# Dequantisation spread on through layer 2's experts, with their inner activations kept by halves of the tokens in a ring of three

## The chip, the core and the metric

The kernel runs on one core of a Trainium2 chip. The metric is the time of one execution on the device, in microseconds (us); lower is better. The engines of a core run each their own instruction stream and wait for each other through semaphores: TensorE (PE, matmuls), VectorE (DVE), ScalarE (ACT), GpSimd (POOL) and SyncE (SP, which here only issues DMA transfers).

## What is computed

A stack of four layers on x of 4 x 256 tokens x 512. Each layer adds a cross-attention to a context of 4 x 64 tokens and then a feed-forward part. The two parts that matter here are layer 2's mixture of three experts and layer 3's feed-forward, whose weights are first quantised to NF4 and dequantised:

```python
# layer 2, feed-forward: all three experts, for all tokens
pre = einsum('bsd,edf->ebsf', h, w1) + b1
act = stack([tanh(pre[0]), gelu(pre[1]), silu(pre[2])])
expert_out = einsum('ebsf,efd->ebsd', act, w2) + b2
# two of them are chosen for each batch and weighed for each token

# layer 3, feed-forward: for each of w1, w2 (1376 x 512), w3 (512 x 1376)
flat = w.reshape(-1, 64)
absmax = max(abs(flat), axis=1)
idx = searchsorted(bounds, flat / absmax)
dq = NF4_CODE[idx] * absmax
h = silu(x @ dq1.T) * (x @ dq2.T)
out = h @ dq3.T
```

The other parts are attention of 16 heads in layer 0, a ternary FFN in layer 0, attention straight to the context in layers 1 and 2, a routed low-rank FFN in layer 1, and attention of 32 heads in layer 3.

## The kernel before

All tokens stay in SBUF as eight tiles of 128 (x), and as a transposed copy in two parts, high and low (xT), in two halves of 512 tokens. A product of full precision is three passes over the high and low parts. So a product of a 512-deep contraction with 128 x 512 outputs is 12 matmuls (L1636). PE writes to a round of seven PSUM banks; an eighth, NF_BANK, belongs to the dequantisation.

`schedule()` writes out one list of steps. Every engine walks this list and does its own part of each step, in order, so an engine that waits holds back all that stands behind it in its stream. Steps named here: `scores0`, `turn0`, `pv0` and `q0` are layer 0's attention; `up0` and `down0` its FFN; `stats` normalises half of x on DVE (L1141 to L1163) and `turn` transposes it on PE (L1661), with a copy of the high part on ACT and the low part on DVE. `gate2` and `moe` make the experts' gates. `hid2(e, c, hf)` is one product of expert e: chunk c of 128 inner features, half hf of the tokens. ACT applies the function into `hf2` (L1048), DVE casts it into `h2` (L1464) and POOL subtracts for the low part (L820). `out2(e, t)` is the second product for token tile t, which DVE adds to x with the gate's factor (L1472, L1473). `k3`, `v3` and `q3` begin layer 3; ACT copies k3 and v3 out of PSUM (L893). `turn(6, hf)` needs the small weight lnw, which POOL loads in `stats(6, 1)`.

The dequantisation of layer 3's weights is independent of x and runs as background. 33 jobs `nf_max` find the block maxima of row tiles (L1550). Then 33 items (three matrices, eleven tiles each) are done. For each, SP loads the weights and the broadcast maxima and reciprocals (`nf_load`, L765 and L767), DVE scales (L1575) and does 15 steps `nf` (L1581, one comparison times a constant each, into a ring of six buffers `nf_y`), PE sums them by 15 matmuls `nf_sum` (L1977) into NF_BANK, four steps behind, DVE closes the item (`nf_end`, L1591) and SP stores it to DRAM (`nf_store`, L773).

`with_background()` inserts these jobs between the first step `v0` and the first step whose name is BACKGROUND_END, in proportion to `room()` of the steps passed: each `nf` costs 1 and each `nf_max` 1.2, and room() is the time that a product leaves, as a table says (2.6 for a product of 12 full matmuls). Weights come through `staging` to a ring of five `slots`: SP loads a chunk two ahead of its split, ACT makes the high part (L903) and POOL the low part (L813). SP issues these loads, the item loads and the stores in one queue.

The tensors of the later stages share memory: h2 and the small tensors of the gate lie where the dequantisation's buffers were. So gate2 and the small loads before it wait until the last item is stored.

## Time and profile before

| | us |
|---|---|
| median of the runs (3, 1707.07 to 1708.24) | 1707.35 |
| the profiled execution | 1711.2 |
| its span, first to last instruction | 1709.4 |
| PE busy | 1443.9 |
| DVE busy | 1083.9 |
| ACT busy | 458.6 |
| POOL busy | 296.5 |

The mean granted clock of TensorE is 0.893 of full speed. Ends of matmuls are modelled in the records, so a busy PE isn't always a PE at its peak. The chain that ended last is followed back from the last instruction, at each step to what released it; its shares say on which engine and line the time of a stretch stands. A line of the form `start us, us, engine line op out<-in xcount [idle before <-releaser]` is a piece of the timeline.

### The profile page before, as it was taken

What the parts mean: (1) busy time and instruction counts of PE and PEld (TensorE: products, weight loads), DVE (VectorE), ACT (ScalarE), POOL (GpSimd) and SP (SyncE); (2) the same over time, 40 slices, a digit from 0 to 9 for tenths busy, and PEclk for the clock granted to TensorE, in tenths of its full rate; (3) what the DMA queues carried; (4) which work ended last, traced back from release to release, by engine and by line L of the source; (5) the groups of instructions that cost most, each with busy time, mean ns of one, the idle gap of its engine ahead of it and who ended that gap; (6) DMA issues with size and microseconds to landing.
All of it is one profiled execution on the core that took longest, in us unless ns stands there. A gap on an engine that the chain in (4) does not pass through costs nothing.

```text
span 1709.4 us, 18898 instructions
## 1 busy us (share of the span) xinstructions
PE 1443.9 (84%) x6489; PEld 1131.2 (66%) x6489; DVE 1083.9 (63%) x2489; ACT 458.6 (27%) x994; POOL 296.5 (17%) x170
## 2 busy tenths in 40 slices
PE   6569999998999898899646878858999778789998
PEld 5347776776677667688545767747887546567786
DVE  4556876767777666948886756554446399944142
ACT  3223423332343333313131202101221333322010
POOL 4101111111111111202021002111543121012120
PEclk9779999999999999999855699557999889899999
DMA  5521232322232212222001112200112000001011
GB/s 184 159 77 46 80 82 68 82 74 58 64 89 71 75 50 69 72 66 67 25 26 46 42 40 60 63 18 1 50 49 62 26 25 1 1 27 60 16 36 49
DMA packets 99407, 96.40 MB, mean 56 GB/s; under 512 B 13138, under 2 KB 72418, under 8 KB 99314
## 3 DMA queue, kind: packets, MB, share of 16 engines
q1 hardware_dynamic: 98802, 94.35, 19.0%
q8 instruction: 54, 0.88, 0.2%
q0 software_dynamic: 512, 0.85, 0.2%
q14 instruction: 39, 0.32, 0.1%
HBM read 84.34 MB, written 10.82 MB: 56 GB/s over the span
## 4 chain that ended last, share of the span: by engine, by line
PE 62%; DVE 25%; issue 4%; ACT 4%; DMA 2%; SPq 1%; POOL 1%; DVEq 0%; ACTq 0%; POOLq 0%
PE bank L1636 48%; PE bank L1977 5%; PE bank L1728 4%; DVE nf_y L1581 3%; DVE st L1141 2%; DVE xn L1159 1%; PE bank L1661 1%; DVE xT L1118 1%; PE bank L1718 1%; DVE mx L1192 1%; DVE mx L1498 1%; ACT e L936 1%; DMA nf_w<-in_L_w 1%; DVE sm L1510 1%; SPq L767 1%
## 5 line engine op out<-in xcount | busy, mean ns | idle before, releaser
L1636 PE MATMUL bank<-xT,slots 128*128 128x512 f32 (+1 forms) x1920 | 467.6, 402 | 9.6 <-DVE xT L1118 7.8
L1636 PEld LDWEIGHTS bank<-xT,slots 128*128 128x128 f32 (+1 forms) x1920 | 354.8, 186 | 109.0 <-issue 8.9
L813 POOL TENSOR_TENSOR slots<-staging,slots 128x1024 fp32r<-128x1024 f32 (+4 forms) x97 | 230.5, 2379 | 1103.0 <-ACT slots L903 1103.0
L1581 DVE TENSOR_SCALAR nf_y<-nf_w 128x512 fp32r<-128x512 f32 (+2 forms) x495 | 232.2, 496 | 29.0 <-PE bank L1977 28.0
L1636 PE MATMUL bank<-slots,h 128*128 128x512 f32 (+1 forms) x728 | 178.8, 405 | 20.1 <-DVE h L1248 13.9
L1977 PE MATMUL bank<-nf_y,nf_d 128*128 128x512 f32 (+2 forms) x495 | 170.6, 429 | 10.3 <-DVE nf_y L1581 8.0
L1636 PEld LDWEIGHTS bank<-slots,h 128*128 128x128 f32 (+1 forms) x728 | 140.8, 194 | 56.1 <-DVE h L1248 14.8
L903 ACT ACTIVATE slots<-staging 128x1024 fp32r<-128x1024 f32 (+4 forms) x97 | 98.1, 1018 | 189.9 <-PE bank L1636 174.2
L936 ACT ACTIVATE e<-bank,mx 128x320 f32<-128x320 f32 x128 | 66.4, 523 | 271.1 <-DVE mx L1195 254.0
L1977 PEld LDWEIGHTS bank<-nf_y,nf_d 128*128 128x128 f32 (+1 forms) x495 | 95.3, 197 | 47.0 <-issue 15.5
L1214 DVE TENSOR_TENSOR x<-bank,x 128x512 f32<-128x512 f32 x72 | 49.7, 690 | 110.9 <-PE bank L1636 110.6
L1728 PE MATMUL bank<-eT,v 128*96 128x256 f32 (+1 forms) x384 | 112.0, 414 | 1.5 <-ACT eT L946 1.5
L1118 DVE TENSOR_TENSOR q<-bank,q 96x256 fp32r<-96x256 f32 (+1 forms) x96 | 48.8, 508 | 77.3 <-ACT q L888 76.8
L1636 PE MATMUL bank<-slots,q 96*128 96x512 f32 x384 | 95.3, 397 | 0.7 <-DVE q L1118 0.7
L1718 PE MATMUL bank<-ident,e 128*128 128x128 f32 x256 | 50.6, 294 | 44.5 <-ACT e L936 22.4
L1636 PEld LDWEIGHTS bank<-slots,q 96*128 96x128 f32 x384 | 71.6, 188 | 18.6 <-issue 2.1
L1728 PEld LDWEIGHTS bank<-eT,v 128*96 128x96 f32 (+1 forms) x384 | 58.2, 172 | 37.6 <-issue 25.3
L1661 PE MATMUL bank<-ident,xn 128*128 128x128 f32 x256 | 49.6, 360 | 31.9 <-DVE xn L1159 31.6
L1636 PE MATMUL bank<-k,q 96*128 96x320 f32 x384 | 69.6, 317 | 5.7 <-ACT e L936 4.4
L1718 PEld LDWEIGHTS bank<-ident,e 128*128 128x128 f32 x256 | 35.0, 151 | 53.7 <-ACT e L936 30.6
L1636 PEld LDWEIGHTS bank<-k,q 96*128 96x128 f32 x384 | 61.9, 192 | 13.0 <-ACT e L936 4.7
L1661 PEld LDWEIGHTS bank<-ident,xn 128*128 128x128 f32 x256 | 42.8, 189 | 39.2 <-issue 34.7
(246 smaller groups left out, 1897.8 us busy)
## 6 DMA issues: line engine op xcount, KB each, us to landing
staging<-in_L_wqkT SPq DMA_DIRECT2D x16, 480.0 KB, 3.8
nf_out<-nf_w SPq DMA_DIRECT2D x30, 256.0 KB, 2.1
staging<-nf_out SPq DMA_DIRECT2D x30, 256.0 KB, 2.8
staging<-in_L_woT SPq DMA_DIRECT2D x16, 384.0 KB, 3.5
staging<-in_L_w SPq DMA_DIRECT2D x12, 512.0 KB, 4.0
nf_a<-nf_max SPq DMA_DIRECT2D x40, 128.0 KB, 3.6
nf_r<-nf_rcp SPq DMA_DIRECT2D x40, 128.0 KB, 3.4
nf_w<-in_L_w SPq DMA_DIRECT2D x15, 256.0 KB, 4.4
```

What stands on the lines that cost most here:

```text
L813: g.tensor_tensor(lo, split_source(i), hi.bitcast(FP32), ALU.subtract).then_inc(*sig.mark("weight_low", i))
L903: sc.activation(weight(name, 0), split_source(i), ACT.Copy).then_inc(*sig.mark("weight_high", i))
L936: sc.activation(e0[:, (2 * n + i) % E0_RING], psum(("scores0", n, i))[:, 0:KEYS0], ACT.Exp, scale=HD0 ** -0.5, bias=mx[:, n % 4, 2 + i:3 + ...
L1118: v.tensor_tensor(dst, src, hi.bitcast(FP32), ALU.subtract).then_inc(*sig.mark(f"{stage}_low", key))
L1141: ins = v.bn_stats(st[:, t], x[:, t])
L1214: v.tensor_tensor(x[:, t], src, x[:, t], ALU.add).then_inc(*sig.mark(*mark))
L1581: v.tensor_scalar(nf_y[0:rows, i % STAIR_RING, 0:size], w_, bound, first, compare, ALU.mult)\
L1636: ins = mm(dst, l_, r_, start=i == 0, stop=i == len(passes) - 1)
L1661: ins = nc.tensor.transpose(bank[:, i * P:(i + 1) * P], xn[:, i, c * P:(c + 1) * P], ident[:])
L1718: nc.tensor.transpose(b0[:, (2 * k + i) * P:(2 * k + i + 1) * P], e0[:, (2 * n + i) % E0_RING, k * P:(k + 1) * P], ident[:])
L1728: ins = mm(bank[0:HD0, 0:S], v0[0:p, t, g * HD0:(g + 1) * HD0], eT0[0:p, n % 2, k], start=k == 0, stop=k == 2)
L1977: mm(banks[NF_BANK][0:rows, 0:size], nf_d[0:rows, j - 1, 0:rows], nf_y[0:rows, i % STAIR_RING, 0:size], start=j == 1, stop=j == NPART).the ...
```

## The change

BACKGROUND_END becomes "k3": the jobs are spread from v0 to the end of the experts, over more steps and so more thinly. The dequantisation's buffers live until then; the tensors of layer 3's attention take their place. Hence the waits for the last nf4 store move from gate2 (ACT, DVE) and from the small loads (POOL) to `k3(0)` on ACT and to the load of lnw on POOL. h2 no longer fits with both parts of two experts for all tokens. It holds three halves: slot (2e + hf) mod 3. The experts' steps are grouped by half: first the hid2 of (0, 0), (0, 1) and (1, 0), then an out2 group of four tiles, then the next hid2 group, and so on. DVE's cast of group r waits for the out2 group r - 3.

```diff
-BACKGROUND_END = "gate2"
+H2_RING = 3
+BACKGROUND_END = "k3"
...
-    steps += [("hid2", 0, 0, 0), ("turn", 5, 1), ("hid2", 0, 0, 1)]
+    steps += [("hid2", 0, 0, 0), ("turn", 5, 1), ("hid2", 0, 1, 0)]
     steps += [("gate2", t) for t in range(TPH, TILES)]
-    for i in range(2 * (KT - 1)):
-        steps += [("moe", i)] * (i < 4) + [("hid2", 0, 1 + i // 2, i % 2)]
-    steps += [("hid2", 1, c, hf) for c in range(KT) for hf in range(2)]
-    for e in range(MOE):
-        steps += [("out2", e, t) for t in range(TPH)]
-        if e == MOE - 1:
+    hidden = [[("hid2", e, c, hf) for c in range(KT)] for e in range(MOE) for hf in range(2)]
+    outer = [[("out2", e, t) for t in range(hf * TPH, (hf + 1) * TPH)] for e in range(MOE) for hf in range(2)]
+    for i, s in enumerate(hidden[0][2:] + hidden[1]):
+        steps += [("moe", i)] * (i < 4) + [s]
+    steps += hidden[2]
+    for i, s in enumerate(outer):
+        steps += s + (hidden[i + H2_RING] if i + H2_RING < len(hidden) else [])
+        if i == len(outer) - 2:
             steps.append(("stats", 6, 0))
-        steps += [("out2", e, t) for t in range(TPH, TILES)]
-        if e + 2 < MOE:
-            steps += [("hid2", e + 2, c, hf) for c in range(KT) for hf in range(2)]
...
-        nfs.close()
...
-        h2 = sb("h2", [P, 2, 2, KT, TOK], F32R, l)
+        h2 = sb("h2", [P, H2_RING, 2, KT, HALF], F32R, l)
...
+        nfs.close()
...
                 elif kind == "stats" and args == (5, 1):
...
-                    for q in range(2):
-                        pool.wait_ge(*sig.when(f"nf4_stored{q}", 3 * FT - 2 + (3 * FT - q) % 2))
...
                 elif kind == "stats" and args == (6, 1):
...
+                    for q in range(2):
+                        pool.wait_ge(*sig.when(f"nf4_stored{q}", 3 * FT - 2 + (3 * FT - q) % 2))
                     small_loads([], [("lnw", lnw[:], a["L3_lnw"])])
...
             def k3_(c):
+                if c == 0:
+                    for q in range(2):
+                        act.wait_ge(*sig.when(f"nf4_stored{q}", 3 * FT - 2 + (3 * FT - q) % 2))
                 keep("k3", c, kr3[:, c], psum(("k3", c))[:, 0:B * CTX])
...
             def hid2(e, c, hf):
-                i = (e * KT + c) * 2 + hf
+                i, r = hid2_no(e, c, hf), 2 * e + hf
                 dve.wait_ge(*sig.when("hid2_value", (e, c, hf)))
-                if e >= 2:
-                    dve.wait_ge(*sig.when("out2_product", (e - 2, TILES - 1)))
-                v.tensor_copy(h2[:, e % 2, 0, c, hf * HALF:(hf + 1) * HALF], hf2[:, i % 2])\
+                if r >= H2_RING:
+                    e_, h_ = divmod(r - H2_RING, 2)
+                    dve.wait_ge(*sig.when("out2_product", (e_, (h_ + 1) * TPH - 1)))
+                v.tensor_copy(h2[:, r % H2_RING, 0, c], hf2[:, i % 2])\
                     .then_inc(*sig.mark("h2_high", (e, c, hf)))
```

The lines of the changed kernel stand two to four further down: L1977 is L1980 there, L1581 is L1583, L1636 is L1638.

PE around the gate (`gw,xT` is gate2, `nf_y,nf_d` a background sum, `ctxN,eT` the end of layer 2's attention), before:

```order
L1790 MATMUL bank<-ident,e 64x128 x2
L1636 MATMUL bank<-ctxN,eT 128x512 x6
L1977 MATMUL bank<-nf_y,nf_d 96x512 x6
L1636 MATMUL bank<-gw,xT 128x4 x48
L1636 MATMUL bank<-xT,slots 128x512 x12
L1661 MATMUL bank<-ident,xn 128x128 x16
```

and with the change:

```order
L1638 MATMUL bank<-ctxN,eT 128x512 x6
L1980 MATMUL bank<-nf_y,nf_d 128x512
L1638 MATMUL bank<-gw,xT 128x4 x12
L1980 MATMUL bank<-nf_y,nf_d 128x512
L1638 MATMUL bank<-gw,xT 128x4 x12
L1980 MATMUL bank<-nf_y,nf_d 128x512
L1638 MATMUL bank<-gw,xT 128x4 x12
L1980 MATMUL bank<-nf_y,nf_d 128x512
L1638 MATMUL bank<-gw,xT 128x4 x12
L1980 MATMUL bank<-nf_y,nf_d 128x512
L1638 MATMUL bank<-xT,slots 128x512 x12
L1980 MATMUL bank<-nf_y,nf_d 128x512 x2
```

The six sums that stood before the gate are one, and sums stand between the gate's products from there on.

PE at the end of the experts (`slots,h` is out2, `ctxT,slots` k3, `slots,ctxT` v3, `ident,xn` turn(6, 0)), before:

```order
L1636 MATMUL bank<-xT,slots 128x512 x96
L1636 MATMUL bank<-slots,h 128x512 x192
L1636 MATMUL bank<-ctxT,slots 128x256 x48
L1636 MATMUL bank<-slots,ctxT 64x128 x48
L1661 MATMUL bank<-ident,xn 128x128 x16
```

and with the change, from the sums ahead of out2(2, 6) on:

```order
L1980 MATMUL bank<-nf_y,nf_d 96x512 x2
L1638 MATMUL bank<-slots,h 128x512 x12
L1980 MATMUL bank<-nf_y,nf_d 96x512 x2
L1638 MATMUL bank<-slots,h 128x512 x12
L1980 MATMUL bank<-nf_y,nf_d 96x512 x6
L1638 MATMUL bank<-ctxT,slots 128x256 x48
L1638 MATMUL bank<-slots,ctxT 64x128 x48
L1663 MATMUL bank<-ident,xn 128x128 x16
```

Six sums stand between the last product of out2 and k3.

DVE at the same place (`y<-bank,b2b` and `x<-y,cf,x` add one out2 tile, `rt<-x` reports that half of x is done), before, from out2(2, 6) on:

```order
L1472 TENSOR_TENSOR y<-bank,b2b 128x512
L1473 SCALAR_TENSOR_TENSOR x<-y,cf,x 128x512
L1472 TENSOR_TENSOR y<-bank,b2b 128x512
L1473 SCALAR_TENSOR_TENSOR x<-y,cf,x 128x512
L1229 COPY rt<-x 1x1
L1172 SCALAR_TENSOR_TENSOR xT<-bank,lnw,xT 128x512 x4
```

and with the change:

```order
L1583 TENSOR_SCALAR nf_y<-nf_w 96x512 x2
L1474 TENSOR_TENSOR y<-bank,b2b 128x512
L1475 SCALAR_TENSOR_TENSOR x<-y,cf,x 128x512
L1583 TENSOR_SCALAR nf_y<-nf_w 96x512 x2
L1474 TENSOR_TENSOR y<-bank,b2b 128x512
L1475 SCALAR_TENSOR_TENSOR x<-y,cf,x 128x512
L1232 COPY rt<-x 1x1
L1583 TENSOR_SCALAR nf_y<-nf_w 96x512
L1593 SCALAR_TENSOR_TENSOR nf_w<-bank,nf_a 96x4x128
L1175 SCALAR_TENSOR_TENSOR xT<-bank,lnw,xT 128x512 x4
```

Two background steps stand before each add, one step and the item's last operation behind the report and before the turn.

## Rows read from the trace of the kernel before

**Rows 1.** The page's first line: the span.

```profile
span 1709.4 us, 18898 instructions
```

**Rows 2.** Busy time of each engine by stretch: attention, then experts.

```profile
core 0: us, PE busy (x) PEld busy (x) DVE busy (x) ACT busy (x) POOL busy (x), PEclk, DMA share, GB/s
135.00:640.00 505.00, 476.73 (x2304) 357.03 (x2303) 364.05 (x877) 179.40 (x483) 73.93 (x31) 0.98 0.26 71
1200.00:1300.00 100.00, 100.00 (x436) 81.42 (x435) 44.85 (x56) 23.41 (x29) 46.16 (x28) 1.00 0.17 53
```

**Rows 3.** The same view for L1581, the background step, alone (x count).

```profile
135.00:640.00 505.00, 161.60 (x326) 0.98 0.26 71
640.00:800.00 160.00, 24.32 (x65) 0.95 0.25 70
800.00:1134.00 334.00, 42.04 (x93) 0.72 0.14 40
```

**Rows 4.** The chain that ended last, shares by line, in the same four stretches.

```profile
by line: PE bank L1636 12.0%; DMA nf_w<-in_L_w 10.5%; POOL slots L813 6.8%; DVE nf_m L1550 5.7%; PE bank L1728 5.2%; DMA nf_a<-in_L_w 4.6%; issue 3.9%; DMA x<-in_x 3.3%; PE bank L1661 3.2%; DVE mx L1192 2.9%; ACT slots L903 2.9%; DVE st L11
...
by line: PE bank L1636 40.2%; PE bank L1728 11.7%; PE bank L1977 11.4%; DVE nf_y L1581 6.9%; PE bank L1718 3.3%; DVE mx L1192 2.9%; issue 2.9%; ACT e L936 2.7%; SPq L767 2.0%; DVE mx L1195 2.0%; DVE q L1118 1.9%; ACT q L888 1.8%; PE bank L1
...
by line: PE bank L1636 78.2%; PE bank L1977 9.1%; issue 3.0%; DVE xT L1118 1.6%; DVE xn L1159 1.0%; DVE f L1237 0.9%; DVE f L1236 0.9%; DVE f L1238 0.9%; DVE st L1141 0.7%; ACT slots L903 0.6%; DVE f L1235 0.5%; DVE f L1260 0.4%; ACT f L967
...
by line: PE bank L1636 36.0%; issue 5.6%; DVE nf_y L1581 5.2%; PE bank L1977 4.5%; DVE st L1141 4.3%; DVE xT L1118 3.6%; DVE xn L1159 3.1%; PE bank L1661 2.6%; DVE f L1236 2.1%; DVE f L1238 2.1%; DVE f L1237 2.1%; PE bank L1829 1.8%; DVE f 
```

**Rows 5.** SP's queue in time; DVE's waits, 135 to 640 us.

```profile
569.97 5.87 SPq L767 DMA_DIRECT2D nf_a<-nf_max  x10
...
DVE nf_w L1575 <- DMA nf_r<-nf_rcp: 14.2, 6, 4.7
```

**Rows 6.** Instructions in time (start, us), 1130 to 1165 us, before the experts.

```profile
1130.78 2.87 PE L1977 MATMUL bank<-nf_y,nf_d 96*96 96x512 f32 x6
...
1131.62 0.14 DVE L1229 COPY rt<-x 1x1 f32<-1x1 f32 x1
...
1134.60 2.44 DVE L1141 BATCH_NORM_STATS2 st<-x 128x6 f32<-128x512 f32 x4
...
1164.23 0.94 PE L1636 MATMUL bank<-xT,slots 128*128 128x512 f32 x3 [2.24 <-DVE xT L1118]
```

**Rows 7.** PE in time; groups (busy, mean ns); durations (ns, minimum/median/maximum).

```profile
1221.43 22.56 PE L1636 MATMUL bank<-slots,h 128*128 128x512 f32 x96
...
L820 POOL TENSOR_TENSOR h<-hf,h 128x512 fp32r<-128x512 f32 x24 | 30.8, 1285 | 64.2 <-DVE h L1464 64.2
...
L1473 DVE SCALAR_TENSOR_TENSOR x<-y,cf,x 128x512 f32<-128x512 f32 x24 | 27.1, 1128 | 0.8
...
L1464 DVE CAST h<-hf 128x512 fp32r<-128x512 f32 x24 | 15.1, 627 | 50.7 <-ACT hf L1048 50.7
...
L1473 DVE SCALAR_TENSOR_TENSOR x<-y,cf,x x24: 752/752/2427, 1225.2 to 1320.1; 128x512 f32<-128x512 f32 x24
...
L1581 DVE TENSOR_SCALAR nf_y<-nf_w 128x512 fp32r<-128x512 f32 x326 | 161.7, 519 | 10.7 <-PE bank L1977 9.9
...
L1581 DVE TENSOR_SCALAR nf_y<-nf_w x495: 337/417/2581, 120.5 to 1131.7; 128x512 fp32r<-128x512 f32 x150, 128x384 fp32r<-128x384 f32 x10, 96x512 fp32r<-96x512 f32 x5
```

**Rows 8.** Instructions in time, end of the experts, 1300 to 1326 us.

```profile
1300.94 0.14 DVE L1229 COPY rt<-x 1x1 f32<-1x1 f32 x1
...
1310.43 6.16 PE L1636 MATMUL bank<-ctxT,slots 128*128 128x256 f32 x48
...
1314.92 0.69 DVE L1472 TENSOR_TENSOR y<-bank,b2b 128x512 f32<-128x512 f32 x1
...
1319.34 0.91 PE L1636 MATMUL bank<-slots,ctxT 128*64 128x128 f32 x12 [0.71 <-DVE x L1473]
...
1322.21 0.14 DVE L1229 COPY rt<-x 1x1 f32<-1x1 f32 x1
...
1325.42 2.72 ACT L888 ACTIVATE xT<-bank,lnw 128x512 fp32r<-128x512 f32 x4 [1.11 <-DMA lnw<-in_L_lnw]
```

More of the change, by code:

```diff
@@ L683, in stair, with hid2_no @@
             return n * NPART + j - 1
+        def hid2_no(e, c, hf):
+            return (2 * e + hf) * KT + c
         def nf_size(m, f):
@@ L817, in hid2 @@
                 pool.wait_ge(*sig.when("h2_high", (e, c, hf)))
-                i = (e * KT + c) * 2 + hf
-                cs = slice(hf * HALF, (hf + 1) * HALF)
-                g.tensor_tensor(h2[:, e % 2, 1, c, cs], hf2[:, i % 2], h2[:, e % 2, 0, c, cs].bitcast(FP32),
-                                ALU.subtract).then_inc(*sig.mark("h2_low", (e, c, hf)))
+                i, h = hid2_no(e, c, hf), h2[:, (2 * e + hf) % H2_RING]
+                g.tensor_tensor(h[:, 1, c], hf2[:, i % 2], h[:, 0, c].bitcast(FP32), ALU.subtract).then_inc(*sig.mark("h2_low", (e, c, hf)))
             def keys3(n, b, c):
@@ L1027, in gate2 @@
                 if t == 0:
-                    for q in range(2):
-                        act.wait_ge(*sig.when(f"nf4_stored{q}", 3 * FT - 2 + (3 * FT - q) % 2))
                     act.wait_ge(*sig.when("pool_gate", "pad"))
@@ L1040, in hid2 @@
             def hid2(e, c, hf):
-                i = (e * KT + c) * 2 + hf
+                i = hid2_no(e, c, hf)
                 act.wait_ge(*sig.when("hid2_product", (e, c, hf)))
@@ L1044, in hid2 @@
                 if i >= 2:
-                    e_, r_ = divmod(i - 2, 2 * KT)
-                    act.wait_ge(*sig.when("h2_low", (e_, r_ // 2, r_ % 2)))
+                    r_, c_ = divmod(i - 2, KT)
+                    act.wait_ge(*sig.when("h2_low", (r_ // 2, c_, r_ % 2)))
                 func = (ACT.Tanh, ACT.Gelu, ACT.Silu)[e]
@@ L1379, in gate2 @@
                 if t == 0:
-                    for q in range(2):
-                        dve.wait_ge(*sig.when(f"nf4_stored{q}", 3 * FT - 2 + (3 * FT - q) % 2))
                     dve.wait_ge(*sig.when("gw_high", 0))
@@ L1893, in out2 @@
                 bank = claim(("out2", e, t), ("out2_added", (e, t)))
-                pairs = [([h2[:, e % 2, q, k, t * P:(t + 1) * P] for q in range(2)], [w[k // 2][q][:, k % 2] for q in range(2)])
+                h, i = h2[:, (2 * e + t // TPH) % H2_RING], t % TPH
+                pairs = [([h[:, q, k, i * P:(i + 1) * P] for q in range(2)], [w[k // 2][q][:, k % 2] for q in range(2)])
                          for k in range(KT)]
```

1 line of the change is left out of this document (removed).

## The prediction

> **What bounds the kernel now.** The profiled execution took 1711.2 us, its span is 1709.4 us [rows 1], and the median of the runs is 1707.35 us; I work out a difference against the profiled execution and subtract it from the median. I read the busy times by stretch first: layer 0's attention (135 to 640 us) has PE busy 476.73 of 505 us, DVE 364.05; the experts (1200 to 1300) have PE busy 100 of 100 us, DVE only 44.85 [rows 2]. So the idle DVE is in the experts, and so is the fullest PE. The background is a DVE step (L1581) and a PE matmul (L1977), 495 of each. It stands in the first 1134 us and nowhere later [rows 3]. Last I read its share of the chain that ended last, by stretch [rows 4].
>
> **What the change moves.** The jobs are spread in proportion to room(). The eligible steps hold 612.6 units of room before; 8 gate2 of 1.2 and 48 products of 2.6 add 134.4. The bill is 33 x 1.2 + 495 = 534.6, so density falls from 0.87 to 0.72 jobs per unit. Counted in the two programs' orders, layer 0's attention has 337 steps before and 269 after (68 fewer), the first FFN up to its second down pass 71 and 58 (13 fewer), from there to gate2 87 and 72 (15 fewer), gate2 and experts 0 and 96.
>
> **What the thinned stretches give.** The price of one step is the chain's share by the steps there. Attention: L1977 11.4%, L1581 6.9%, L767 2.0% of 505 us, together 102.5 us for 326 steps, 0.314 us each [rows 3, 4]; 68 fewer give 21.4 us. FFN: 9.1% of 160 us for 65 steps, 0.224 us; 13 give 2.9. After it: 5.2% and 4.5% of 334 us, 32.4 us for 93 steps, 0.35 us; 15 give 5.2. Sum **29.5 us**. The lower end is that a dropped step frees only its matmul: 96 in 22.56 us, 0.235 us each [rows 7], so 96 x 0.235 = 22.6 us. I take the chain's price, because DVE steps and DMA issue do stand in the chain beside the matmul.
>
> Start, 0 to 135 us: the 33 block maxima (L1550) and the row loads they wait for are 5.7 + 10.5 + 4.6% of 135 us, 28 us of chain [rows 4]. Their number stays, but 18% more real steps lie between them. 18% of 28 is **5 us**; ends 0 (the same loads are merely waited for elsewhere) and 10.
>
> Loads: an item of the third matrix is loaded by one DMA and 20 broadcasts, and ten of these take 5.87 us of issue on SP's queue, so the item takes 12 [rows 5]. The load stands 7 steps ahead of its use. A step takes 505/326 = 1.55 us now, so 10.9 us against 12 and the landing; DVE waited 14.2 us in 6 cases [rows 5]. At 269 steps it takes about 1.9 us, 13.3 us ahead. I take **4 us** beyond what the shares hold already; ends 0 and 12.
>
> Gate: x was done for its second half at 1131.62, but DVE first ended the background's last item, which waited for six sums on PE, and began stats(5,1) at 1134.60; stats starts up to **2.9 us** sooner [rows 6]. The small loads on POOL start 5 us sooner and stay hidden, since the gate's weights wait for DVE, behind stats. What follows there is the same chain. hid2 now takes the first half of the tokens again after turn(5,1), so PE's wait of 2.24 us for xT [rows 6] is covered: **2.2 us**. Together the gains are 29.5 + 5 + 4 + 2.9 + 2.2 = 43.6 us.
>
> **What the experts pay.** By the order 89 sums stand before out2(2,4), 30 of them 384 wide: 59 x 0.235 + 30 x 0.176 = **19 us** of a PE that has no gap [rows 2, 7]. Ends: 15 if some fall into waits of the gate, and 21 if the narrow ones cost as much as the wide. The first ones fall where the granted clock is low: 6 sums took 2.87 us, 0.48 each [rows 6], so some 8 of them add **2 us**. Two background steps before stats(6,0): **0.8 us**. Loads of items 29 and 32 stand three to four products ahead, about 9.5 to 13 us, against 12 to 14 us needed, and SP first waits for weight splits; PE runs on until it meets a sum of the late item: **4 us**, ends 0 and 8. The ring of three costs nothing: each h2 slot is rewritten only after a group of out2 that PE has ended already, and out2 of a half has four products between itself and the last hid2 that feeds it, some 11 us against ACT's activation, DVE's cast of 0.6 and POOL's 1.3 us [rows 7]. That cover would cost 2.5 us a group, six groups, if it were gone.
>
> End of the experts, the largest single loss. Count from 1300.94, the end of DVE's out2(2,3). Before, k3 starts on PE at 1310.43 under DVE's stats and adds, done(6,1) is at 1322.21, lnw lands, and ACT turns at 1325.42, 24.5 us after the start [rows 8]. Now six background steps (0.42 each) stand among DVE's last four adds. DVE also meets two POOL splits, which already stretched L1473 there, from its median of 0.75 us to 2.43 at most [rows 7]. So done(6,1) comes at about +24.3 instead of +21.3. Behind it stands step 15, and PE's sixth sum waits for that before k3: k3 starts at +25.2 instead of +9.5. k3 takes 6.2 us, v3 3.6, the first transposes 0.8: ACT turns at +35.7. That is **11 us** later. Queued behind the sum on PE are k3, v3 and the turn of layer 6; ACT's k3 copies and POOL's lnw load wait for the last nf4 store, at about +32, and so are not last. Ends: 6 (POOL's splits fall elsewhere) and 20 (the clock falls while PE waits).
>
> Costs: 19 + 2 + 0.8 + 4 + 11 = 36.8 us. Against 43.6 that is **7 us faster**: 1704 for the profiled execution, 1700.5 for the median.
>
> **A rule weighed.** L1581 has a median of 417 ns and a maximum of 2581 ns; its mean in the attention is 519 ns, with POOL busy 73.93 of 505 us [rows 2, 7]. In the experts POOL is busy 46.16 of 100 us.
> The Trainium skill (SBUF — State Buffer, "SBUF: two separate sides") says that VectorE and GpSimd share a port pair that one instruction holds to its end while the other is blocked. That speaks against putting background DVE steps where POOL splits h2; the stretched L1473 agrees, 2.427 us beside a median of 0.752 [rows 7]. What it would give is the second rival.
>
> **Rivals.** (1) *The waits for loads go almost wholly.* The attention and the start keep no wait for rows or broadcasts: 12 us instead of 4, 10 instead of 5: 13 us more, **1687.5**. For it: DVE waits 14.2 us for broadcasts, and 28 us of the start are chain [rows 4, 5]. Against: PE was not idle through all of it.
> (2) *DVE becomes the bound of the experts.* There it does 24 adds of 0.69 + 1.13 and 24 casts of 0.63 us [rows 7, 8], and for 6 items the scaling and the closing operation, 1.4 us by my estimate: 67 us. PE needs 48 x 2.82 + 19 = 154 us. So DVE decides once a step costs (154 - 67)/89 = 0.98 us. Scaling its excess over the median with POOL's share, 0.10 x 46/15, gives 0.73 us: below, but not by much, and casts wait in order for ACT. At 1.15 us the stage is 15 us longer: **1716**.
> (3) *The saved waits were covered.* Start and loads give nothing: 9 us lost, **1709**, no difference. For it: PE is busy 94% of the attention [rows 2].
> That the change does not do what it says is excluded by the order: 96 steps stand in the experts.
>
> **How the numbers follow.** Forecast 1700.5 with 0.40, its own range 1693 to 1706; rival 1 0.19; rival 3 0.19; rival 2 0.22. The range 1687 to 1714 cuts off half of rival 1 and the top of rival 2, 0.2 in all. About 0.2% (3.4 us) can be told from no change. Faster by more: 0.37 of the forecast's 0.40 and rival 1's 0.19, 0.56; within: 0.03 + 0.19 = 0.22; slower: 0.22.
>
> **What would show it.** The attention ends some 25 to 30 us sooner (start and loads within it). Gate to the first expert product keeps its length but for 2 us. The experts are 25 us longer, PE still full; if PE has gaps there that end at L1583 or at h2, rival 2 holds. Between the last out2 and the first q3, PE waits for DVE's last step, and k3 stands behind it. I am wrong if the thinned attention gives under 15 us, or if L1583 has a mean over 0.9 us after gate2.

## The result and the profile after

| | kernel before | changed kernel |
|---|---|---|
| median of 4 runs, us | 1707.8 (1707.07 to 1708.97) | 1735.1 (1733.94 to 1736.69) |
| profiled execution, us | 1711.2 | 1734.67 |
| its span, us | 1709.4 | 1732.9 |

The ratio is 1.016, with a 95% interval of 1.0142 to 1.0177: 27 us slower, where 7 us faster was forecast, and outside the range of 1687 to 1714. Beside three experiments in a later session the same kernel gave 1730.3 us (1724.9 to 1737.0), a ratio of 1.0125 (1.0081 to 1.0169). The sign is safe, the size uncertain by some 5 us. All medians and ratios are of executions in the faster of two states; of all runs only two of the kernel before with 2 broadcasts (1782.75 and 2367.23 us) fell in the slower one and are left out.

The page's first line, the busy time of each engine in the attention and in the experts, and then the same view for L1583 alone, the background step (L1581 before):

```profile
span 1732.9 us, 18901 instructions
...
core 0: us, PE busy (x) PEld busy (x) DVE busy (x) ACT busy (x) POOL busy (x), PEclk, DMA share, GB/s
132.00:623.00 491.00, 463.58 (x2224) 346.53 (x2223) 334.63 (x804) 178.76 (x481) 73.70 (x31) 0.96 0.24 66
1190.00:1300.00 110.00, 109.81 (x482) 89.77 (x481) 84.69 (x123) 23.74 (x29) 49.50 (x29) 1.00 0.26 69
...
132.00:623.00 491.00, 131.09 (x265) 0.96 0.24 66
623.00:790.00 167.00, 21.70 (x54) 0.94 0.20 56
790.00:1126.00 336.00, 35.68 (x76) 0.71 0.15 43
1126.00:1305.00 179.00, 60.85 (x83) 0.89 0.21 56
```

Against [rows 2, 3]: the attention has 61 steps fewer in its stretch (265 for 326), but is only 14 us shorter, and its granted clock is 0.96 instead of 0.98. In the experts TensorE is still full at the upper level of its clock, so the background costs there what its sums take.

To see where the time goes, all traces are laid on each other by TensorE's own products: every matmul that is not of the background has the same number in every kernel. The table gives when some of them start, as a difference to the kernel before, with the first one of each trace set equal. The forecast's column is its terms added up to that place; the last three columns belong to experiments below.

```
                            before,  fore-  changed  scales  tail steps  ring only,
product no., place          us       cast   kernel   first   out         scales first
 500  attention, early      171.1    -5      -6.9    -10.7   -10.0       -5.0
2250  end of attention      620.0   -30     -16.8    -26.6   -23.0       -8.5
3000  end of feed-forward   839.7   -33     -10.6    -30.6   -26.3       -8.6
3250  routers               957.6           -15.3    -34.1   -30.0       -8.2
3750  last before the gate 1096.5   -38.5    -5.9    -24.0   -19.5       -9.7
4000  experts, early       1184.8   -43.6    -6.3    -23.5   -20.2      -12.2
4500  third expert's last  1304.8   -18     +11.2     -4.7   -16.4      -12.0
4750  next layer's scores  1369.4    -7     +20.9     +6.6    -6.0      -11.9
5750  last feed-forward    1646.3    -7     +22.0     +7.8    -4.7      -10.7
```

From the experts on, the costs came out near the forecast (27 us instead of 37 from product 4000 to 4750; but 15 sums already stand between the gate and product 4000, and the gain of 5 us forecast for that stretch doesn't show there, so from product 3750 on it is 27 us instead of 32). It is the gain in front of them that is missing: 6 us instead of 38.5 at product 3750. Two places stand out, the feed-forward layer, which gives 6 us back, and the stretch from the routers to the gate, which gives back 9.

The feed-forward layer, instructions in time (start, us; in brackets the idle time before, and what ended it):

```profile
716.82 0.69 DVE L1593 SCALAR_TENSOR_TENSOR nf_w<-bank,nf_a 128x512 f32<-128x512 f32 x1 [2.36 <-PE bank L1980]
...
717.43 1.42 DVE L1583 TENSOR_SCALAR nf_y<-nf_w 128x512 fp32r<-128x512 f32 x4
717.54 0.34 SPq L777 DMA_DIRECT2D nf_out<-nf_w  x1
...
719.86 1.77 DVE L1583 TENSOR_SCALAR nf_y<-nf_w 128x512 fp32r<-128x512 f32 x5 [1.01 <-PE bank L1980]
...
721.48 0.34 SPq L769 DMA_DIRECT2D nf_w<-in_L_w3T  x1
721.87 5.84 SPq L771 DMA_DIRECT2D nf_a<-nf_max  x10
...
735.02 0.69 DVE L1577 TENSOR_TENSOR nf_w<-nf_w,nf_r 128x512 f32<-128x512 f32 x1 [9.77 <-DMA nf_r<-nf_rcp]
...
737.26 1.62 PE L1980 MATMUL bank<-nf_y,nf_d 128*128 128x512 f32 x3 [5.78 <-DVE nf_w L1593]
```

SP's queue stores an item at 717.54 and issues the load of the next third-matrix item only at 721.48, once the store has landed. Ten broadcasts of maxima take 5.84 us of issue, ten more of scales follow, and VectorE stands still for 9.77 us until the scales are there. TensorE runs dry for 5.78 us behind it. A like wait of 6.75 us is at 265 us, in the attention. The sum of VectorE's waits for scales is 28.1 us in 6 here and was 29.9 in 9 before; the kernel before has one of 8.4 us too, at 765 us. So the waits themselves don't tell what they cost, and two experiments below take them away on either schedule.

### The profile page after: what moved, and what is told of

Read it like the earlier page. It is cut to its first block, busy times and chain, and to the rows that moved or that the text cites. A ratio compares the mean times of both kernels' runs of the same rounds, so it can differ in the third digit from the quotient of the medians.

```text
span 1732.9 us, 18901 instructions
## 1 busy us (share of the span) xinstructions
PE 1459.6 (84%) x6489; PEld 1143.8 (66%) x6489; DVE 1103.8 (64%) x2489; ACT 458.7 (26%) x994; POOL 298.7 (17%) x170
## 4 chain that ended last, share of the span: by engine, by line
PE 62%; DVE 24%; issue 5%; ACT 3%; DMA 2%; SPq 2%; POOL 1%; ACTq 0%; DVEq 0%; POOLq 0%
PE bank L1638 48%; PE bank L1980 5%; PE bank L1730 4%; DVE nf_y L1583 3%; DVE st L1144 2%; SPq L771 2%; DVE xn L1162 1%; PE bank L1720 1%; PE bank L1663 1%; DVE xT L1121 1%; DVE mx L1500 1%; DVE mx L1195 1%; ACT e L938 1%; POOL slots L817 1%; DVE sm L1512 1%
## 5 line engine op out<-in xcount | busy, mean ns | idle before, releaser
L1638 PE MATMUL bank<-xT,slots 128*128 128x512 f32 (+1 forms) x1920 | 467.1, 400 | 11.0 <-DVE xT L1175 5.9
L1638 PEld LDWEIGHTS bank<-xT,slots 128*128 128x128 f32 (+1 forms) x1920 | 353.6, 185 | 110.4 <-issue 10.6
L1583 DVE TENSOR_SCALAR nf_y<-nf_w 128x512 fp32r<-128x512 f32 (+2 forms) x495 | 258.1, 545 | 29.8 <-PE bank L1980 28.7
L1638 PE MATMUL bank<-slots,h 128*128 128x512 f32 (+1 forms) x728 | 188.7, 416 | 21.3 <-DVE h L1251 15.1
L1980 PE MATMUL bank<-nf_y,nf_d 128*128 128x512 f32 (+2 forms) x495 | 174.7, 430 | 16.1 <-DVE nf_y L1583 10.3
L1638 PEld LDWEIGHTS bank<-slots,h 128*128 128x128 f32 (+1 forms) x728 | 145.5, 201 | 58.1 <-DVE h L1251 16.0
L1980 PEld LDWEIGHTS bank<-nf_y,nf_d 128*128 128x128 f32 (+1 forms) x495 | 96.4, 199 | 56.1 <-DVE nf_y L1583 22.5
L1730 PE MATMUL bank<-eT,v 128*96 128x256 f32 (+1 forms) x384 | 117.2, 430 | 1.7 <-ACT eT L948 1.7
L1638 PE MATMUL bank<-slots,q 96*128 96x512 f32 x384 | 95.1, 396 | 1.2 <-DVE q L1121 1.2
L1638 PEld LDWEIGHTS bank<-slots,q 96*128 96x128 f32 x384 | 71.8, 188 | 19.1 <-issue 2.3
L1638 PE MATMUL bank<-k,q 96*128 96x320 f32 x384 | 73.2, 328 | 10.8 <-ACT e L938 6.9
L1638 PEld LDWEIGHTS bank<-k,q 96*128 96x128 f32 x384 | 65.2, 201 | 17.7 <-ACT e L938 7.4
L1720 PEld LDWEIGHTS bank<-ident,e 128*128 128x128 f32 x256 | 36.3, 155 | 45.0 <-ACT e L938 23.6
```

The source lines that it names most:

```text
L1583: v.tensor_scalar(nf_y[0:rows, i % STAIR_RING, 0:size], w_, bound, first, compare, ALU.mult)\
L1638: ins = mm(dst, l_, r_, start=i == 0, stop=i == len(passes) - 1)
L1720: nc.tensor.transpose(b0[:, (2 * k + i) * P:(2 * k + i + 1) * P], e0[:, (2 * n + i) % E0_RING, k * P:(k + 1) * P], ident[:])
L1730: ins = mm(bank[0:HD0, 0:S], v0[0:p, t, g * HD0:(g + 1) * HD0], eT0[0:p, n % 2, k], start=k == 0, stop=k == 2)
L1980: mm(banks[NF_BANK][0:rows, 0:size], nf_d[0:rows, j - 1, 0:rows], nf_y[0:rows, i % STAIR_RING, 0:size], start=j == 1, stop=j == NPART).the ...
```

## The experiments

The experiments ran in four sessions; each gives a ratio to the kernel before on the same chip. Its medians there were 1710.6, 1708.35, 1707.7 and 1709.2 us.

### The ring alone, and the background's end alone

Both start from the changed kernel.

```
 # ring alone
-BACKGROUND_END = "k3"
+BACKGROUND_END = "gate2"
 # end at the third expert's product
-BACKGROUND_END = "k3"
+BACKGROUND_END = ("out2", 2, 0)
```

> The changed kernel with the background ending at gate2 again: the jobs stand as densely as before, the experts' steps are grouped by halves and h2 is the ring of three, the waits for the last store stand at k3. If the ring costs nothing and only the spread does, this is 1703 to 1706 us (2.2 us for the covered turn, up to 2.9 at the gate). If the grouping by halves costs PE waits on h2 or on weights, it is 1712 us or more.

Measured: 1708.4 us (1699.3 to 1711.6), ratio 0.9987 (0.9967 to 1.0008). The trace has nothing up to the gate and 5.8 us of gain behind it, where the forecast had 5.1 for the earlier stats and the covered turn. The ring costs nothing. By the medians of all its runs the gain is 2.2 us.

> The changed kernel with the background ending before out2(2, 0) instead of before k3. The end of the experts then has no background step among DVE's last adds and no sum ahead of k3. If that place costs the 12 us that the two traces show, this is 1722 to 1725 us against 1735. If the loss there comes from the grouping or from elsewhere, it stays within 3 us of 1735.

Measured: 1708.25 us (1705.5 to 1710.9), ratio 0.9982 (0.9966 to 0.9998), 27 us less than the changed kernel. By the trace none of it is gained behind the gate: from product 3750 to 4750 this version loses 28 us against the kernel before and the changed kernel 27, since six sums in one piece now cost 4.5 us ahead of the third expert's product, and the gate's stretch (product 3750 to 4000) is 5 us dearer. The whole advantage lies in front of the gate (-33.0 us at product 3750, against -6.0), where the steps stand only a little denser: 9 us of it where the wait of the feed-forward layer is missing, 7 between the routers and the gate, and 15 in the start and the attention, less 4 in between. What makes the 15 is not shown. It has three waits for scales, 15.2 us in all, and none in the feed-forward layer.

### What a background step is worth

From the kernel before, three of the fifteen steps of items 1 to 21 go, with their sums (the second expectation below says sixteen, counting the scaling):

```
+        def left_out(n, j):
+            return 1 <= n <= 21 and j in (3, 8, 13)
...
             def nf(n, m, f, j):
...
+                if left_out(n, j):
...
+                    return
...
             def nf_sum(n, m, f, j):
...
+                if left_out(n, j):
...
+                    return
```

> The kernel before with 63 background steps and their sums left out, 3 of 15 in items 1 to 21, so all in layer 0's attention; nothing is added elsewhere. The dequantised values are not the reference's. This is the thinning alone. By the chain's price of the prediction (0.31 us a step) it is 20 us faster, 1688. By the matmul's price (0.235) 15 us, 1693. If the changed kernel's small gain there is the true price (10 us for 68 steps, 0.15 each, since the clock falls when PE has fewer matmuls) it is 1698 us or more, with a mean granted clock in the attention under 0.98.

Measured: 1697.8 us (1696.9 to 1699.1), ratio 0.9928 (0.99 to 0.9955). 63 steps with their sums are worth 12.8 us, **0.20 us** each; the traces say 12.4 at the end of the attention, where the granted clock is 0.97.

The same with the second part of the edit taken back, so that TensorE makes the 63 sums of stale steps and VectorE doesn't make the steps:

> The kernel before, with the same 63 background steps of VectorE left out as in the run with fewer steps (three of the sixteen of items 1 to 21), but their 63 sums on TensorE kept. This leaves those steps out of the computation. The run with fewer steps was 1697.8 us beside 1710, so a step with its sum was worth some 0.19 us there. Theory A: TensorE sets the pace of the attention, so nearly all of that price is the sum's time on TensorE: this run comes back to 1708 to 1710. Theory B: the price is VectorE's (a step of 0.5 us delays the real VectorE work on which TensorE waits): this run stays at 1697 to 1700. In between, the price is shared in proportion.

Measured: 1709.3 us (1704.2 to 1716.2), ratio 1.0006 (0.9987 to 1.0024). The price is TensorE's, within the interval: 63 steps of VectorE less, of 0.5 us each, are worth nothing there, give or take 4 us.

### What the experts pay

From the version with scales first (below), 13 of 15 steps of items 27 to 32 and their sums are left out, so 78 in all; loads, scaling, closing operation and stores stay.

```
+        def left_out(n, j):
+            return n >= 27 and 1 < j < NPART
```

> The changed kernel with the scales loaded first, and of the last six background items (27 to 32, nearly all behind the gate) 13 of 15 steps and their sums left out, so that part of the dequantisation is not computed; loads, scalings, closing operations and stores of these items stay. It prices what the experts pay. The forecast's terms for these 78 steps: 17 us of sums, 2 for the low clock, nearly all of the 11 us at the end: 28 to 32 us below the 1719 us of the version with scales first, so 1687 to 1691. If a step among the experts costs no more than one in the attention (0.18 us) and the end goes with it, 14 + 11: 1694. If the end stays, because the store and the closing operation make it and not the steps, 1700 to 1704.

Measured: 1705.7 us (1702.1 to 1708.2), 13.1 us below the 1718.75 of that version; ratio to before 0.9977 (0.9964 to 0.999). By the table it is 15.0 us shorter from product 4000 to 4500, where 10 sums stand instead of 78 (41 of them 128x512, 30 128x384 and 7 96x512). That is **0.22 us** for each of the 68, and close to the forecast's own price: 42 wide ones at 0.235 and 26 narrow ones at 0.176 us are 14.4 us. And the end stays: from 4500 to 4750 this version loses 10.4 us, with only two steps of the last item left. The end of the experts in it, in time:

```profile
1304.61 0.40 DVE L1592 TENSOR_SCALAR nf_y<-nf_w 96x512 fp32r<-96x512 f32 x1
1305.07 0.74 PE L1993 MATMUL bank<-nf_y,nf_d 96*96 96x512 f32 x1 [10.66 <-DVE nf_y L1592]
1305.61 8.08 PE L1648 MATMUL bank<-ctxT,slots 128*128 128x256 f32 x48
...
1320.34 1.84 ACT L896 ACTIVATE xT<-bank,lnw 128x512 fp32r<-128x512 f32 x3 [3.47 <-DMA lnw<-in_L_lnw]
```

TensorE waits 10.66 us for one step that stands behind VectorE's stats and last adds, and the next layer's keys are queued behind its sum. In the changed kernel the same place reads:

```profile
1323.81 0.74 PE L1980 MATMUL bank<-nf_y,nf_d 96*96 96x512 f32 x1 [4.72 <-DVE nf_y L1583]
...
1329.65 5.02 POOL L817 TENSOR_TENSOR slots<-staging,slots 128x1024 fp32r<-128x1024 f32 x2 [25.21 <-ACT slots L905]
...
1329.97 0.14 DVE L1232 COPY rt<-x 1x1 f32<-1x1 f32 x1
1330.04 2.38 DVE L1583 TENSOR_SCALAR nf_y<-nf_w 96x512 fp32r<-96x512 f32 x1
...
1332.47 0.47 PE L1980 MATMUL bank<-nf_y,nf_d 96*96 96x512 f32 x1 [2.89 <-DVE nf_y L1583]
1332.78 7.39 PE L1638 MATMUL bank<-ctxT,slots 128*128 128x256 f32 x48
...
1339.33 1.27 ACT L895 ACTIVATE kr<-bank 128x256 f32<-128x256 f32 x4 [8.81 <-DMA nf_out<-nf_w]
...
1340.49 1.05 ACT L905 ACTIVATE slots<-staging 128x1024 fp32r<-128x1024 f32 x1
...
1341.62 2.38 POOL L817 TENSOR_TENSOR slots<-staging,slots 128x1024 fp32r<-128x1024 f32 x1 [6.96 <-ACT slots L905]
...
1342.89 1.93 PE L1663 MATMUL bank<-ident,xn 128*128 128x128 f32 x16
...
1343.94 0.56 POOL L811 DMA_DIRECT2D lnw<-in_L_lnw  x1
...
1346.96 2.42 ACT L890 ACTIVATE xT<-bank,lnw 128x512 fp32r<-128x512 f32 x4 [3.60 <-DMA lnw<-in_L_lnw]
```

The wait is spread over two sums, and the last step took 2.38 us where the median of L1583 is 0.42, beside GpSimd's splits. ACT turns 16.99 us after the mark at 1329.97, where it was 3.21 us before [rows 8]. Keys and values now stand in between, but they are not what ends last: the transposes start at 1342.89, and ACT then still waits 3.60 us for lnw. GpSimd issues that load only at 1343.94, behind a split whose high part ACT makes after its copies of k3; the copies begin when the last store has landed. The version without the steps has the same wait, 3.47 us. No run moves the load of lnw alone, so what it costs is not shown.

### The end, packed

The changed kernel's schedule; the 14 steps that stood behind the start of the third expert's product are placed directly ahead of it.

```
             base = with_background(base, "v0", BACKGROUND_END, jobs)
+            at = base.index(("out2", 2, 0))
+            late = [s for s in base[at:] if s[0].startswith("nf")]
+            base = base[:at] + late + [s for s in base[at:] if not s[0].startswith("nf")]
```

> The changed kernel, its own spacing kept up to the third expert's product; only the background work that stood from there on (14 steps, the last item's sums, its closing operation and its store) is moved directly ahead of that product. Theory of the forecast: the end of the experts is delayed by 10 to 12 us because the last step and its sums stand in front of the next layer's key product, so this run is at 1735 - 12 = 1723 us, and the first product of the next layer stands 10 us sooner against the gate than in the changed kernel. Rival: the run with the background ended there gained 27 us because of the end itself; then this one is at 1710 as well. If 1723, the other 15 us of that gain come from where the loads and steps fall in the first layer.

Measured: 1728.15 us (1726.1 to 1734.7), ratio 1.0131 (1.01 to 1.0163). It looks like 7 us, but the trace says otherwise. Up to that product it has the instructions of the changed kernel, one for one, and is already 8.6 us ahead at product 4000; then it loses 10.6 us at the packed place and gains 10.3 behind the experts. Both theories missed: a burst of the last item costs as much in front of the product as behind it. Here 21 sums stand in one piece for 13.4 us; with the end at the third expert's product and even spacing, it is six for 4.5 us, as ahead of k3 in the changed kernel. The 8.6 us are how far two executions of the same instructions can lie apart.

### Late scales

First an earlier issue of the whole load:

```
-                    if j == NPART // 2 + 1 and n + 1 < len(items):
+                    if j == 5 and n + 1 < len(items):
```

> The changed kernel with each item's load issued after step 5 of the item ahead of it instead of after step 8. If the late loads on SP's queue cost what the chain shows for L771 (some 25 to 30 us in all, in pieces of 10), this is 1715 to 1725 us. If PE would wait for other things there anyway, it is 1732 us or more.

Measured: 1731.0 us (1729.4 to 1732.3), ratio 1.0121 (1.0093 to 1.0149). Three steps more of lead gave almost nothing. VectorE's waits for scales from 132 to 1305 us (us in total, times, longest), first the changed kernel's:

```profile
DVE nf_w L1577 <- DMA nf_r<-nf_rcp: 20.0, 5, 9.8
```

and with the earlier load:

```profile
DVE nf_w L1577 <- DMA nf_r<-nf_rcp: 16.7, 3, 8.6
```

The load can't be issued earlier, since it waits on SP's queue for the landing of the store before it.

Then 2 broadcasts instead of 20 for a third-matrix item, on both kernels:

```
-                    for dr in range(4):
-                        p = 0
-                        while p < w:
...
+                    pairs.append((dst_tile[0:w, 0:D], src[0:4].partition_broadcast(w)))
```

> The changed kernel, with the scales of a third-matrix item brought by 2 broadcasts where there were 20, and so left out in part (the dequantised values are not the right ones); every other instruction stays. Theory A: the waits of VectorE for late scales (6.75 us at 265, 9.77 us at 735, and the granted clock that falls after TensorE stood still) ate what the thinner first layer should have given; then this run is 15 to 22 us below the changed kernel, 1713 to 1720, no VectorE wait over 2 us stands ahead of a third-matrix item, and the granted clock of the attention is back at 0.98. Rival B: the load is late because of the store it waits for, not because of its twenty broadcasts: 1728 to 1733, and the waits stay. Rival C: the waits vanish, but what they delayed was covered: the same time, 1731 to 1735.

> The same edit in the kernel before (2 broadcasts of scales for a third-matrix item where there were 20, so part of them is left out). It tells what the broadcasts cost there. Theory A: the kernel before loses 3 to 4 us in the feed-forward layer and 2 to 6 us in the attention to them, so 1700 to 1706 us, and the distance between this pair shrinks from 27 us to 12 to 17. Theory C: no change, 1708 to 1711.

Measured: 1721.1 us (1717.9 to 1722.4), ratio 1.008 (1.0054 to 1.0107), on the changed schedule; 1705.9 us (1700.3 to 1714.7), ratio 0.9989 (0.9969 to 1.0009), on the one before. The broadcasts cost the changed kernel 9 to 14 us (its two medians are of other sessions), and the kernel before nothing that stands clear of the noise.

Last, a version that computes everything: the scales, which are needed first, are issued first and ahead of the wait for the store, and the maxima, needed at the item's end, last.

```
+                for dst, src in broadcast_rows(nf_r[:], nf_rcp[m], m, f):
+                    sp.dma_start(dst, src).then_inc(*sig.mark(f"nf4_weights{n % 2}", n, 16))
                 if n >= 2:
                     sp.wait_ge(*sig.when(f"nf4_stored{n % 2}", n - 2))
...
-                for dst, src in broadcast_rows(nf_a[:, n % 2], nf_max[m], m, f) + broadcast_rows(nf_r[:], nf_rcp[m], m, f):
-                    sp.dma_start(dst, src).then_inc(*sig.mark(f"nf4_weights{n % 2}", n, 16))
+                for dst, src in broadcast_rows(nf_a[:, n % 2], nf_max[m], m, f):
+                    sp.dma_start(dst, src).then_inc(*sig.mark(f"nf4_bounds{n % 2}", n, 16))
...
             def nf_end(n, m, f):
...
                 dve.wait_ge(*sig.when("nf4_summed", stair(n, NPART)))
+                dve.wait_ge(*sig.when(f"nf4_bounds{n % 2}", n))
```

> The changed kernel, unchanged, beside the next three on the same chip. The kernel with packed end has the same instructions up to the third expert's second product, and was yet 8.6 us ahead of it at the gate in the trace, so two executions of one instruction stream can differ. If that is so, this run spreads over 1726 to 1737 us. If the changed kernel is at 1733 to 1737 here again, packing the end was worth 7 us.

> The changed kernel, every value computed; of an item's load SP's queue issues the ten scale broadcasts first, ahead of its wait for the older item's store, then the weights, and the ten broadcasts of the maxima, which are used sixteen steps later, last and on their own semaphore. Theory A (late scales ate the gain of the first layer): as with two broadcasts, 1718 to 1724 us; the VectorE waits of 6.75 us at 265 and 9.77 us at 735 fall under 3 us. Rival (the store's landing, not the issue of broadcasts, makes the load late): the weights land as late as before, 1728 to 1735.

> The same order of the load, on the version whose background ends ahead of the last expert's product. That version has two waits for scales left in the trace, 5.96 and 8.46 us. If waits for scales cost what theory A says, 1698 to 1704 us, faster than the kernel before by 0.3 to 0.6 %; if what they delay is covered, 1706 to 1710.

> The same order of the load in the kernel before. Two broadcasts instead of twenty gave nothing there (ratio 0.9989), so theory A and its rivals agree on 1705 to 1711; it is there so that the two orders of the load are compared on both schedules.

Measured in one session: changed kernel 1730.3 us; with scales first **1718.75** (1715.4 to 1726.9), ratio 1.0058 (1.0035 to 1.008); end at the third expert's product with scales first 1704.7 (1700.2 to 1708.1), ratio 0.9976 (0.9955 to 0.9996); kernel before with scales first 1705.4 (1699.5 to 1709.0), ratio 0.9982 (0.9965 to 1.0). Late scales cost the changed kernel 12 us by these medians, and the kernel before 2, at the edge of its interval. The four runs of the changed kernel lie in two pairs (1724.9 twice, 1735.7 and 1737.0), so the 12 us are rough. The traces show the places: against the version with scales first, the four traces with the old order of the load on this schedule (the changed kernel twice, the packed end, the earlier load) lose 3 to 7 us between products 500 and 1000 and 6 to 9 between 2600 and 2750, where the two long waits stand. What ended VectorE's idle time before the scaling, in the changed kernel (one releaser for 28.1 us) and with scales first:

```profile
L1577 DVE TENSOR_TENSOR nf_w<-nf_w,nf_r x33: 544/684/1781, 125.7 to 1300.7; 128x512 f32<-128x512 f32 x30, 128x384 f32<-128x384 f32 x2, 96x512 f32<-96x512 f32 x1
its engine sat idle before it (us, times) until:
  DMA nf_r<-nf_rcp: 28.1, 6
```

```profile
L1579 DVE TENSOR_TENSOR nf_w<-nf_w,nf_r x33: 544/682/1781, 119.9 to 1284.5; 128x512 f32<-128x512 f32 x30, 128x384 f32<-128x384 f32 x2, 96x512 f32<-96x512 f32 x1
its engine sat idle before it (us, times) until:
  DMA nf_w<-in_L_w1T: 6.2, 1
  DMA nf_w<-in_L_w3T: 2.3, 1
```

The wait of 6.2 us that is left is that of the first item, at 119.9 us.

Part of what a wait costs is TensorE's clock. Busy time from 250 to 290 us in the changed kernel, around its wait of 6.75 us, and in the version with scales first:

```profile
250.00:270.00 20.00, 15.24 (x75) 10.91 (x74) 9.44 (x27) 6.19 (x17) 2.21 (x1) 0.97 0.21 60
270.00:290.00 20.00, 19.29 (x85) 14.14 (x86) 12.12 (x35) 9.83 (x31) 1.80 (x1) 0.78 0.27 74
```

```profile
250.00:270.00 20.00, 17.71 (x92) 12.33 (x90) 15.62 (x37) 8.64 (x24) 4.31 (x2) 1.00 0.29 84
270.00:290.00 20.00, 20.00 (x103) 15.60 (x103) 13.16 (x37) 6.99 (x23) 0.00 (x0) 1.00 0.17 51
```

After TensorE stood still, the clock granted over the next 20 us is a mean of 0.78 of its upper level, so part of that time is at the lower one: 85 matmuls instead of 103, though TensorE is busy in 19.29 of the 20 us. In the other it stays at the upper level. TensorE is idle 3.2 us longer over the 40 us, and 35 matmuls of some 195 are missing, so by estimate about half of the loss there is the clock. Two more traces of the same instructions have 163 and 169 matmuls in the 40 us (the changed kernel again and the packed end), and the run with 2 broadcasts 196.

### Where the steps fall between the routers and the gate

```
-    out, at, spent, paid, bill = list(steps[:a]), 0, 0.0, 0.0, sum(price)
+    out, at, spent, paid, bill = list(steps[:a]), 0, 0.0, 5.0, sum(price)
```

> The changed kernel with scales first and every background job five steps later, the spacing unchanged. By the traces the changed schedule loses 8 to 10 us between the routers and the gate against the kernel before, where a scaling and a step of VectorE stretched to 2.4 us beside a split of GpSimd stand in a serial chain. If that is the place where the steps fall, it moves by some us here, and the run is 1710 to 1728 with another pattern of waits; if it is the spacing itself, the stretch keeps its 149 us and the run stays at 1717 to 1721.

Measured: 1718.3 us (1717.5 to 1725.1), ratio 1.0069 (1.0046 to 1.0093), the same as without the shift; but from product 3250 to 3750 it takes 141.6 us instead of 149.0 (138.9 in the kernel before). So the loss there comes from the place, not from the spacing, as the one theory had it. The difference is larger than that between executions: seven traces whose steps stand where the changed kernel has them lose 5 to 10 us in that stretch against the kernel before, six of them over 7; this one loses 3. The 7.4 us are lost again elsewhere: 4.5 ahead of the routers, and 3.4 at the end of the experts, where the five jobs for which no place is left stand in front of k3 as well (11 sums in one piece instead of 6). One of the two places at which they differ is a chain of VectorE between products 3650 and 3750 (4.2 us), in the version with scales first:

```profile
1059.33 0.68 DVE L1579 TENSOR_TENSOR nf_w<-nf_w,nf_r 128x512 f32<-128x512 f32 x1
1059.79 2.44 POOL L819 TENSOR_TENSOR slots<-staging,slots 128x1024 fp32r<-128x1024 f32 x1 [18.17 <-ACT slots L907]
1060.05 2.80 DVE L1585 TENSOR_SCALAR nf_y<-nf_w 128x512 fp32r<-128x512 f32 x2
...
1065.63 2.92 PE L1641 MATMUL bank<-ctxN,eT 64*128 64x512 f32 x6 [4.88 <-DVE eT L1123]
```

and five steps later:

```profile
1060.07 0.75 DVE L1585 TENSOR_SCALAR nf_y<-nf_w 128x512 fp32r<-128x512 f32 x2
...
1063.94 2.93 PE L1641 MATMUL bank<-ctxN,eT 64*128 64x512 f32 x6 [1.31 <-DVE eT L1123]
```

Two steps take 2.80 us beside a split of GpSimd and 0.75 us ahead of it; with the scaling, TensorE waits 4.88 instead of 1.31 us. The other place is between products 3350 and 3450 (4.5 us): there an item's scaling and closing operation stand ahead of VectorE's L1353, for which TensorE waits 4.6 instead of 2.9 us, and the granted clock is 0.89 instead of 0.95. The Trainium skill (SBUF — State Buffer, "SBUF: two separate sides") has GpSimd and VectorE, when it runs in a two-port mode or reads two inputs from SBUF, lock each other out of a shared pair of ports for a whole instruction. The rows agree: the two steps begin 0.26 us after the split and end 0.62 us behind it.

### Versions that beat both kernels

> Ring of three and halves, the background ending at the gate as before, scales loaded first. The two edits gave 2 us (ring) and 2 us (load order on the kernel before) by themselves; if they add, 1703 to 1706; 5 us or more below the kernel before would make it the fastest.

> Scales loaded first, the background ending ahead of the first expert's product instead of the third's, so about half of the moved steps return to the first layer. If a step costs about the same in both places, only the ends matter: 1700 to 1706, as the version that ends at the third expert's product (1704.7). If the experts' steps cost more (0.24 against 0.18 us), 2 to 3 us less than that.

Measured: **1701.95 us** (1695.3 to 1709.3), ratio **0.9954** (0.9934 to 0.9974), for the ring and the halves with the background ending at the gate, as before, and scales first. With the end at the first expert's product: 1703.5 us (1696.6 to 1714.2), ratio 0.9979 (0.9956 to 1.0001). The first is the fastest that computes everything, and the only such one clear of both kernels by more than 0.2%; the three versions lie within 3 us of each other by their medians (two sessions), wherever the background ends. So the fastest version keeps the ring and the halves of the change and not its spreading. The ring and the order of the load add up or do a little more: -0.13% and -0.18% by themselves, -0.46% together, with intervals of 0.2% on each side.

## Why the prediction was wrong

The prediction named its own sign of being wrong, under 15 us from the thinned attention. From product 500 to 2250 it gave 10.

- **The loads** are the step that failed most. It said that, with the steps 18% further apart, a load seven steps ahead of its use has 13.3 us against 12, so 4 us are gained. Two things were left out: steps are not spaced in time (in the feed-forward layer nine of them went by in 4.2 us, from 717.43 on), and SP issues the load only once the store before it has landed, 3.9 us after its issue here. The waits were fewer and longer: 6.75 us in the attention, where the longest of [rows 5] had been 4.7, and 9.77 in the feed-forward layer. The kernel before had 8.4 us there, but by the run with scales first nothing waited for that (5.2 us of gain at the layer's start and at its end). By the run with scales first the loss in the changed kernel is 12 us by the medians, and 15.8 by the traces of that session. With the 4 us not gained, 16 us of the error.
- **The price of a step** was mis-sized: 0.314 us from the chain's shares [rows 4], 0.20 by the run with fewer steps, and all of it the sum's. The 96 moved steps were worth 19 us, not 29.5. The prediction's lower end, the matmul alone at 0.235, was the better price: leaving out only VectorE's part gave nothing. This is 10 us.
- **Between routers and gate** the forecast took the gain through. The changed schedule loses 9 to 10 us there, at two places where an item's start stands in a serial chain of VectorE, one of them beside a split. This term was missing; it depends on the place.
- **Start:** 5 us forecast, 6.9 by the table: right in the main. There are 22% more real steps between two jobs, not 18% (134.4 of 612.6 units), which alone makes it 6. **Gate and turn:** 5.1 forecast, 5.8 measured with the ring alone: right.
- **The experts:** 25.8 us forecast for sums, clock, steps before stats and late loads. Measured are 17 from product 3750 to 4500 with the gate's gain in it; with that gain at the 5.1 forecast, the cost is 22. The sums were priced rightly (15.0 us measured for 68, 14.4 by the forecast's prices). The 4 us too many are as much as the term for the late loads 29 and 32, which cost nothing visible (longest wait of that stretch 1.3 us).
- **End of the experts:** 11 us forecast, 9.7 in the changed kernel, 11.3 with scales first. The last step behind VectorE's adds, with k3 queued behind its sum, begins it, as described; the burst of six steps doesn't, as the run without them shows. That the number fits is in part luck. Counted from the same mark (1310.71 here), ACT turns at +36.3, +35.7 forecast, but k3 starts at +22.1 instead of +25.2 and takes 7.4 instead of 6.2 us, and what ACT waits for last is the load of lnw, issued at +33.2, of which the prediction said that it is not last.
- **Rivals.** VectorE did not become the bound: L1583 has a mean of 0.73 us after the gate (60.85 us for 83), the 0.73 that the prediction had worked out, and below the 0.98 from which it would decide. That the waits for loads go was the opposite of what happened, and would have been right with another order of the load. That saved waits were covered held in part: VectorE's steps were, to within 4 us.

Added up against the profiled execution: 1704 forecast + 16 (loads) + 10 (price) + 10 (routers to gate) - 4 (experts) - 1 (end) - 2 (start) = 1733, for 1734.7 measured. The 2 us left are within what two executions of this kernel differ by.

The deeper fault: a step costs 0.20 us where it leaves and 0.22 us where it arrives, and the two can't be told apart. Moving 96 of them can't pay by itself, so that only the edges count: the start and the gate gave 5 to 7 us each, and the late scales, the place between routers and gate and the end of the experts cost 9 to 12 each.

## What to carry to other kernels

Before you move filler work from one stretch of a full TensorE to another, price one unit in both, by leaving out a few dozen in each: if the two prices are equal, the move is worth nothing, and its edges decide. Look in the new order for the last unit in front of the next stage, and for the prefetches whose lead was counted in units of work rather than in time. Where a load consists of many small transfers, issue first what is used first, and put only the transfer that overwrites a buffer behind the wait for that buffer.

## What the runs showed of the hardware that was not expected

The same instruction stream came 8.6 us apart at product 4000 in two executions (changed kernel and the one with its end packed), and four runs of the changed kernel in one session spread over 12 us (1724.9 to 1737.0), where four of another session lay within 3; the four lie in two pairs 11 us apart. Ten broadcasts from one queue took 5.84 us to issue, 0.58 each. And 63 VectorE instructions of 0.5 us, taken out of a stretch in which VectorE is busy 70% of the time, changed nothing that stands clear of 4 us.
